# Reciprocals and layer-norm powers moved from VectorE and GpSimd to logarithm, exponential and correction steps on ScalarE and GpSimd, with new program orders

## The chip, the core and the metric

The kernel runs on one core of a Trainium2 chip. A core has five engines that run side by side, each with its own instruction queue taken in order: TensorE (PE in the profile; PEld are its weight loads), VectorE (DVE), ScalarE (ACT), GpSimd (POOL) and SyncE (SP), which here only starts DMA transfers. Engines wait for each other through semaphores. The metric is the device time of one execution in microseconds (us); lower is better.

## What is computed

The input is 32 images of 56 x 56 positions with 32 channels. A binarized 3x3 convolution is added to the image, then a linear-attention block and a mixture of experts, each behind a layer norm over the 32 channels:

```
x = x + conv(sign(batchnorm(groupnorm(x))), sign(W) * scale)
t = x as tokens                       # 3136 tokens per image
z = layernorm(t)                      # (t - mean) / sqrt(var + 1e-5)
q, k = elu(z Wq + bq) + 1, elu(z Wk + bk) + 1;  v = z Wv + bv      # 16 heads of 32
kv = sum over tokens of k*cos (x) v and of k*sin (x) v
denom = 1 / (q*cos . sum(k*cos) + q*sin . sum(k*sin) + 1e-5)       # per token and head
t = t + (q*cos . kv_cos + q*sin . kv_sin) * denom  @ dense_w + dense_b
z = layernorm(t)
t = t + sum over the 2 best of 8 experts of gate * (z We + be)
```

Two things in it matter here: `1 / sqrt(var + eps)` of both layer norms, 112 x 28 values per image each, and the reciprocal of the attention's denominator, two pieces of 128 x 224 values per image.

## The kernel before, in words

Each image is cut into seven tiles of four token groups (28 slots of 112 tokens). All work on an image is split into steps with short names, and a table `ORDER` gives each engine a list of times for each kind of step. A period is 14 units; times outside 0 to 14 mean that the step belongs to an earlier or later image than the one at hand. `iteration` sorts the table into one list per engine, so in the steady state every engine repeats a fixed list in which the steps of up to six images are interleaved. Nothing is decided at run time: an engine does its steps in that order and waits where a semaphore isn't there yet. The table also fixes which step uses which of three PSUM ring slots (`ring`) and the one shared bank (`misc`).

The steps that the change touches:

- `XC` centers the first layer norm's input on PE and ACT; `SM1` on DVE sums the squares (L993) and makes the variance `varr` (L996). `S2` and `SM2` do the same for the second layer norm, with the same line L996 for `varr`.
- `PN1` and `PN2` on POOL raise `varr` to the power -0.5 into `rstd` (L819), and multiply it into `xn` (L825). After that PE transposes `xn` (`ZT`, `ZU`, L572), ACT and DVE split it into two half-precision parts `zhl` (L717, L1007), and SP sends it through DRAM into `z`.
- `DN` and `SU` on PE make the attention's denominator, in two pieces per image; ACT adds a constant and stores it as `den` (L745).
- `RC` on DVE takes the reciprocal of `den` in place (L1032); `RC` on ACT rounds it to half precision, `r_high` (L749); `RL` on POOL stores the difference of the two (L850) into `rs`, and `RH` on ACT copies the rounded part beside it (L753).
- `R` and `RP` on PE spread `rs` over heads (L636); DVE (`R`, L1035) and, from a copy `spread_r` by ACT (L759), POOL (`RP`, L838) multiply it into `qbuf`.
- `K` and `Q` on PE (L582, L610) make keys and queries; ACT takes the exponential (L722, L727) and DVE finishes elu + 1 (L1012, L1018). `F` are the experts' products: PE (L670), gating on DVE (L1097), three pairwise sums on POOL (L877, L880, L883).

POOL's two uses of the power, and DVE's reciprocal, read before:

```
nc.gpsimd.tensor_tensor(rstd[ln][:, :], varr[ln][:, :], power[0:PT, 0:SLOTS], ALU.pow)
v.reciprocal(den[:, 0:HALFW], den[:, 0:HALFW])
act.activation(r_high[:, :], den[:, 0:HALFW], ACT.Copy)
```

## Time and profile before

| | |
|---|---|
| median of three runs | 2406.02 us (2404.33 to 2406.26) |
| the profiled execution's own time | 2404.97 us |
| its span, from first to last instruction | 2403.2 us |
| PE busy | 2183.1 us (91%) |
| DVE busy | 2062.3 us (86%) |
| POOL busy | 1839.2 us (77%) |
| ACT busy | 1516.3 us (63%) |

Busy time is the union of an engine's instructions, so overlapping ones count once. The span has three parts: a prologue and fill in which the first images enter, a steady state that repeats image by image, and a drain. The shares of the whole span mix these, so what one step is worth is read from the steady part. The TensorE clock is granted at full speed (1.00, 2.4 GHz) all through the steady part.

### The profile page before, as it was taken

How to read it: one execution, taken by the hardware profiler on the slowest of the kernel's cores; microseconds unless marked ns; L12 is line 12 of the kernel's file. 1: busy time of each engine (PE TensorE's matmuls, PEld its weight loads, DVE VectorE, ACT ScalarE, POOL GpSimd, SP SyncE). 2: the span in 40 equal slices, each digit the busy share in tenths (PEclk: the TensorE clock that was granted, in tenths of full speed). 3: DMA queues.
4: the chain of work that ended last, by engine and by line, in shares of the span. 5: the costliest groups of instructions: out<-in, count | busy, mean ns of one | idle time of the engine just before them, and what ended most of it. 6: DMA issues, size and time to landing. Idle time of an engine off the chain costs nothing.

```text
span 2403.2 us, 44296 instructions
## 1 busy us (share of the span) xinstructions
PE 2183.1 (91%) x15620; PEld 1098.5 (46%) x15620; DVE 2062.3 (86%) x2694; ACT 1516.3 (63%) x2757; POOL 1839.2 (77%) x1553
## 2 busy tenths in 40 slices
PE   5379999999999999999999999999999999999972
PEld 5224444444444444444444444444444444444441
DVE  5257899999999999999999999999999999999853
ACT  0157767667666666666667666676676766766630
POOL 0314688888888888888888888888888888888786
PEclk8589999999999999999999999999999999999985
DMA  9442323323343243344432343344322333332111
GB/s 235 121 55 39 62 50 59 68 55 65 72 71 65 55 55 68 57 60 72 72 68 59 51 65 65 52 72 72 72 61 52 58 68 54 66 65 61 28 28 34
DMA packets 485705, 156.59 MB, mean 65 GB/s; under 512 B 438688, under 2 KB 472336, under 8 KB 485360
## 3 DMA queue, kind: packets, MB, share of 16 engines
q1 hardware_dynamic: 485488, 153.75, 35.1%
q8 instruction: 129, 2.11, 0.4%
q14 instruction: 88, 0.72, 0.1%
HBM read 95.41 MB, written 51.38 MB: 61 GB/s over the span
## 4 chain that ended last, share of the span: by engine, by line
POOL 35%; PE 25%; DVE 17%; ACT 10%; issue 10%; DMA 3%; SPq 0%; POOLq 0%; ACTq 0%; DVEq 0%
POOL rstd L819 11%; POOL qbuf L838 7%; DVE qbuf L1018 6%; POOL prod L877 5%; ACT ebuf L727 4%; PE ps L619 4%; POOL xn L825 4%; PE ps L645 3%; POOL prod L880 3%; PE ps L593 3%; PE ps L610 3%; PE ps L636 2%; ACT ebuf L722 2%; POOL xcs L833 2%; PE ps L658 2%
## 5 line engine op out<-in xcount | busy, mean ns | idle before, releaser
L727 ACT ACTIVATE ebuf<-ps,small 128x896 f32<-128x896 f32 x448 | 450.3, 1005 | 163.7 <-PE ps L610 150.0
L838 POOL TENSOR_TENSOR qbuf<-spread_r,qbuf 128x896 f32<-128x896 f32 x224 | 469.4, 2096 | 94.4 <-ACT spread_r L759 94.4
L1018 DVE SCALAR_TENSOR_TENSOR qbuf<-ps,ebuf 128x896 f32<-128x896 f32 x448 | 484.9, 1082 | 58.9 <-ACT ebuf L727 58.3
L1012 DVE SCALAR_TENSOR_TENSOR kbuf<-ps,ebuf 128x1024 f32<-128x1024 f32 (+1 forms) x416 | 487.6, 1172 | 48.2 <-ACT ebuf L722 44.7
L722 ACT ACTIVATE ebuf<-ps,small 128x1024 f32<-128x1024 f32 (+1 forms) x416 | 448.0, 1077 | 116.0 <-DVE kbuf L1012 68.2
L593 PE MATMUL ps<-kbuf,xcs 128*64 128x512 f32 (+1 forms) x1600 | 440.4, 611 | 7.7 <-DVE kbuf L1012 4.0
L819 POOL TENSOR_TENSOR rstd<-varr,power 112x28 f32<-112x28 f32 x64 | 307.2, 4800 | 164.9 <-DVE varr L996 164.8
L645 PE MATMUL ps<-qbuf,gmat 128*64 128x224 f32 x3584 | 386.2, 357 | 1.6 <-DVE pbuf L1041 1.0
L645 PEld LDWEIGHTS ps<-qbuf,gmat 128*64 128x64 f32 x3584 | 248.5, 136 | 154.6 <-issue 51.3
L1097 DVE TENSOR_TENSOR prod<-ps,gate 112x1024 f32<-112x1024 f32 x224 | 273.0, 1220 | 52.2 <-PE ps L670 37.1
L877 POOL TENSOR_TENSOR prod<-prod 112x512 f32<-112x512 f32 x224 | 285.6, 1275 | 20.9 <-DVE prod L1097 20.3
L582 PE MATMUL ps<-wk,z 128*128 128x512 f16 (+1 forms) x800 | 244.2, 384 | 23.4 <-issue 14.0
L1035 DVE TENSOR_TENSOR qbuf<-ps,qbuf 128x896 f32<-128x896 f32 x224 | 243.4, 1087 | 23.3 <-PE ps L636 20.0
L636 PE MATMUL ps<-rs,sel 128*128 128x448 f16 x896 | 241.6, 358 | 20.1 <-DVE qbuf L1018 8.5
L610 PE MATMUL ps<-z,wq 128*128 128x448 f16 x896 | 246.1, 356 | 8.1 <-DVE qbuf L1018 6.9
L759 ACT ACTIVATE spread_r<-ps 128x896 f32<-128x896 f32 x224 | 205.3, 916 | 72.1 <-PE ps L636 43.7
L619 PE MATMUL ps<-qbuf,dmat 128*32 128x448 f32 x1792 | 234.8, 555 | 2.2 <-DVE qbuf L1018 1.9
L880 POOL TENSOR_TENSOR prod<-prod 112x256 f32<-112x256 f32 x224 | 163.2, 729 | 17.6
L593 PEld LDWEIGHTS ps<-kbuf,xcs 128*64 128x64 f32 (+1 forms) x1600 | 101.2, 136 | 120.6 <-issue 74.6
L670 PE MATMUL ps<-we,z 128*112 128x256 f16 x896 | 145.0, 288 | 10.4 <-DVE prod L1097 10.4
L636 PEld LDWEIGHTS ps<-rs,sel 128*128 128x128 f16 x896 | 67.5, 99 | 182.3 <-issue 63.1
L717 ACT ACTIVATE zhl<-ps 128x448 f16<-128x448 f32 (+1 forms) x128 | 63.5, 497 | 134.5 <-PE ps L572 134.5
(132 smaller groups left out, 3129.0 us busy)
## 6 DMA issues: line engine op xcount, KB each, us to landing
z<-zd SPq DMA_DIRECT2D x256, 196.0 KB, 3.8
zd<-zhl SPq DMA_DIRECT2D x64, 392.0 KB, 2.4
qbuf<-in_x SPq DMA_DIRECT2D x16, 784.0 KB, 9.5
xt<-in_x SPq DMA_DIRECT2D x256, 49.0 KB
xd<-xn SPq DMA_DIRECT2D x128, 98.0 KB, 2.9
out<-ffn SPq DMA_DIRECT2D x256, 49.0 KB
xkt<-xd SPq DMA_DIRECT2D x32, 384.0 KB, 6.6
shifted<-nat SPq DMA_DIRECT2D x128, 52.6 KB, 5.3
```

The lines of the kernel that those rows point to most:

```text
L593: mm = pe.matmul(kt_bank[64 * k:64 * k + 64, :], xcs[0:w, i, :, :].rearrange("p a c -> p (a c)"), kbuf[0:w, m.at(KS, n) % 2, DH * k:DH * k ...
L610: mm = pe.matmul(o[:, k, 0:G * PT].rearrange("p (g t) -> p g t", g=G), wq16[:, 128 * (k0 + k):128 * (k0 + k) + 128], z1[:, m.par, :, j, :] ...
L619: mm = pe.matmul(o[32 * j:32 * j + 32, 0:HW4], dmat[:, m.par, c, :, :].rearrange("p a h -> p (a h)"), qbuf[:, c, 4 * h + j, :], start=(c = ...
L636: mm = pe.matmul(o[:, k, 0:HW4], sel16[:, 128 * a:128 * a + 128], rs[:, j // 4, :], start=True, stop=True)
L645: mm = pe.matmul(o[64 * v:64 * v + 64, 0:2 * PT].rearrange("p (a t) -> p a t", a=2), gmat[:, m.par, c, :, :].rearrange("p a o -> p (a o)") ...
L722: act.activation(ebuf[0:w, 0, 0:DH * c].rearrange("p (a b) -> p a b", a=c), o[0:w, 0:c, :], ACT.Exp, bias=minus_one[0:w, :]).then_inc(kexp ...
L727: act.activation(ebuf[:, 1, 0:2 * G * PT].rearrange("p (a b) -> p a b", a=2), o[:, :, 0:G * PT], ACT.Exp, bias=minus_one).then_inc(qexp_ma ...
L819: nc.gpsimd.tensor_tensor(rstd[ln][:, :], varr[ln][:, :], power[0:PT, 0:SLOTS], ALU.pow)\
L838: nc.gpsimd.tensor_tensor(qbuf[:, 2:4, n, :], spread_r[:, :, :], qbuf[:, 2:4, n, :], ALU.mult)\
L877: nc.gpsimd.tensor_tensor(p[:, :, 0:4 * C], p[:, :, 0:4 * C], p[:, :, 4 * C:], ALU.add)\
L1012: v.scalar_tensor_tensor(kbuf[0:w, m.at(KS, n) % 2, 0:DH * c].rearrange("p (a b) -> p a b", a=c), o[0:w, 0:c, :], 1.0, ebuf[0:w, 0, 0:DH * ...
L1018: v.scalar_tensor_tensor(qbuf[:, k0:k0 + 2, j, :], o[:, :, 0:G * PT], 1.0, ebuf[:, 1, 0:2 * G * PT].rearrange("p (a b) -> p a b", a=2), AL ...
```

## The change

It replaces the reciprocal on DVE. ACT now takes the logarithm of `den` (into its unused half, named `resid`) and the exponential of its negative, which gives `r_high` directly. A new POOL step `RE` multiplies `den` by `r_high`; a new ACT step `SQ` takes the square of (1.5 minus that); `RL` on POOL subtracts 0.25 and multiplies by `r_high`. It replaces the power on POOL as well: new ACT steps `LV1` and `LV2` take logarithm, exponential and square of `varr`-sized tiles, and POOL corrects the seed with three small instructions. The program loads ACT's function table once, at the start, under a name that holds both functions. And the whole table `ORDER` is a new one, for all five engines.

```
+            nc.scalar.preload_act_table_set("natural_log_exp_and_others")
...
                     act.activation(den[:, 0:HALFW], o[:, 0:HALFW], ACT.Identity, bias=den_eps).then_inc(den_made, 1)
-                elif kind == "RC":
-                    act.wait_ge(recip_made, m.at(2, n + 1))
+                    act.wait_ge(den_made, m.at(2, n + 1))
+                    act.activation(resid, den_in, ACT.Ln).then_inc(log_made, 1)
+                    act.wait_ge(log_made, m.at(2, n + 1))
                     wait(act, qr_made, m.at(7, -3 if n == 0 else 0))
-                    act.activation(r_high[:, :], den[:, 0:HALFW], ACT.Copy).then_inc(rhigh_made, 1)
+                    act.activation(r_high[:, :], resid, ACT.Exp, scale=-1.0).then_inc(rhigh_made, 1)
+                elif kind == "SQ":
+                    act.wait_ge(resid_made, m.at(2, n + 1))
+                    act.activation(resid, resid, ACT.Square, bias=three_half, scale=-1.0).then_inc(resid_squared, 1)
+                elif kind in ("LV1", "LV2"):
+                    ln = kind == "LV2"
+                    act.wait_ge(var_made[ln], m.at(1, 1))
+                    act.activation(lnv[ln][:, :], varr[ln][:, :], ACT.Ln, scale=SEED * SEED).then_inc(seed_step[ln], 1)
+                    act.wait_ge(seed_step[ln], m.at(2, 1))
+                    act.activation(seed[ln][:, :], lnv[ln][:, :], ACT.Exp, scale=-0.5).then_inc(seed_step[ln], 1)
+                    act.wait_ge(seed_step[ln], m.at(2, 2))
+                    act.activation(newton[ln][:, :], seed[ln][:, :], ACT.Square, scale=SEED).then_inc(seed_made[ln], 1)
...
-                    pool.wait_ge(var_made[ln], m.at(1, 1))
-                    nc.gpsimd.tensor_tensor(rstd[ln][:, :], varr[ln][:, :], power[0:PT, 0:SLOTS], ALU.pow)\
+                    pool.wait_ge(seed_made[ln], m.at(1, 1))
+                    nc.gpsimd.tensor_tensor(newton[ln][:, :], newton[ln][:, :], varr[ln][:, :], ALU.mult)\
+                        .then_inc(newton_step[ln], 1)
+                    pool.wait_ge(newton_step[ln], m.at(2, 1))
+                    nc.gpsimd.tensor_scalar(newton[ln][:, :], newton[ln][:, :], -0.5 * SEED, 1.5 * SEED, ALU.mult, ALU.add)\
+                        .then_inc(newton_step[ln], 1)
+                    pool.wait_ge(newton_step[ln], m.at(2, 2))
+                    nc.gpsimd.tensor_tensor(rstd[ln][:, :], seed[ln][:, :], newton[ln][:, :], ALU.mult)\
                         .then_inc(rstd_made[ln], 1)
...
+                elif kind == "RE":
+                    pool.wait_ge(rhigh_made, m.at(2, n + 1))
+                    nc.gpsimd.tensor_tensor(resid, den_in, r_high[:, :], ALU.mult).then_inc(resid_made, 1)
                 elif kind == "RL":
-                    pool.wait_ge(rhigh_made, m.at(2, n + 1))
+                    pool.wait_ge(resid_squared, m.at(2, n + 1))
+                    nc.gpsimd.tensor_scalar(resid, resid, -0.25, None, ALU.add).then_inc(resid_series, 1)
+                    pool.wait_ge(resid_series, m.at(2, n + 1))
...
-                elif kind == "RC":
-                    dve.wait_ge(den_made, m.at(2, n + 1))
-                    v.reciprocal(den[:, 0:HALFW], den[:, 0:HALFW]).then_inc(recip_made, 1)
```

Of the table, one line each of before and of the change:

```
-        "RC": [10.80, 17.78],
+        "SQ": [8.169, 15.462],
```

Three places of the new order, in the middle of the program.

On GpSimd, from the second layer norm's power to the second piece of the attention's reciprocal; before it reads (L819 are the powers, L825 `xn`, L833 `xcs`, L838 `RP`, L877 to L883 the sums of `F`, L850 `RL`):

```order
L819 TENSOR_TENSOR rstd<-varr,power 112x28 [waits var_made2]
L825 TENSOR_TENSOR xn<-xc,rstd 112x28x31 [waits high_made2,rstd_made2]
L833 TENSOR_TENSOR xcs<-xkt,tabk 128x13x32 [waits ktx_done,xkt_in]
L833 TENSOR_TENSOR xcs<-xkt,tabk 128x13x32
L838 TENSOR_TENSOR qbuf<-spread_r,qbuf 128x2x448 [waits r_copied]
L819 TENSOR_TENSOR rstd<-varr,power 112x28 [waits var_made1]
L825 TENSOR_TENSOR xn<-xc,rstd 112x28x31 [waits xkt_out,high_made1,rstd_made1]
L877 TENSOR_TENSOR prod<-prod 112x4x128 [waits prod_made]
L880 TENSOR_TENSOR prod<-prod 112x4x64 [waits pool_add]
L883 TENSOR_TENSOR ffn<-prod 112x128 [waits pool_add]
```

and of the change the piece from the first layer norm's correction (L846, L849, L852) to `RL` (L885, L888), where L882 is `RE` and L915 to L921 are the sums of `F`:

```order
L846 TENSOR_TENSOR newton<-newton,varr 112x28 [waits seed_made1]
L849 TENSOR_SCALAR newton<-newton 112x28 [waits newton_step1]
L852 TENSOR_TENSOR rstd<-seed,newton 112x28 [waits newton_step1]
L858 TENSOR_TENSOR xn<-xc,rstd 112x28x31 [waits xkt_out,high_made1,rstd_made1]
L882 TENSOR_TENSOR den<-den,r_high 128x224 [waits rhigh_made]
L915 TENSOR_TENSOR prod<-prod 112x4x128 [waits prod_made]
L918 TENSOR_TENSOR prod<-prod 112x4x64 [waits pool_add]
L921 TENSOR_TENSOR ffn<-prod 112x128 [waits pool_add]
L885 TENSOR_SCALAR den<-den 128x224 [waits resid_squared]
L888 TENSOR_TENSOR rs<-den,r_high 128x448 [waits resid_series]
```

The power has become three instructions behind a wait for ACT's seed, and a multiply for `RE` and a small add stand where there was only the subtraction.

On ScalarE, around the first piece of the reciprocal; before (L745 stores `den`, L749 rounds it, L727 and L722 are the exponentials of `Q` and `K`, L777 is `S2`, L753 is `RH`):

```order
L745 ACTIVATE den<-ps,small 128x224 [waits r_made,misc_full]
L727 ACTIVATE ebuf<-ps,small 128x896 [waits q_made,ring_full]
L722 ACTIVATE ebuf<-ps,small 128x1024 [waits k_made,ring_full]
L749 ACTIVATE r_high<-den 128x224 [waits qr_made,recip_made]
L777 ACTIVATE sq<-xc 112x256 [waits piece_summed,centered]
L727 ACTIVATE ebuf<-ps,small 128x896 [waits q_made,ring_full]
L753 ACTIVATE rs<-r_high 64x224 [waits r_made]
```

and of the change (L760 stores `den`, L762 is the logarithm, L765 the exponential, L768 `SQ`, L804 `S2`, L742 and L737 the exponentials of `Q` and `K`, L796 and L798 `T2`, L780 `RH`):

```order
L760 ACTIVATE den<-ps,small 128x224 [waits r_made,misc_full]
L762 ACTIVATE den<-den 128x224 [waits den_made]
L765 ACTIVATE r_high<-den 128x224 [waits qr_made,log_made]
L804 ACTIVATE sq<-xc 112x256 [waits piece_summed,centered]
L742 ACTIVATE ebuf<-ps,small 128x896 [waits q_made,ring_full]
L768 ACTIVATE den<-den,small 128x224 [waits resid_made]
L737 ACTIVATE ebuf<-ps,small 128x1024 [waits k_made,ring_full]
L796 ACTIVATE t<-ps 112x256 [waits misc_full]
L798 ACTIVATE mean<-ps 112x8
L780 ACTIVATE rs<-r_high 64x224 [waits r_made]
```

ACT now does three instructions in a row for each piece, and stops once more, at L768, for GpSimd.

On VectorE, where the two variances are made in the changed order (L1035; L1032 is the first layer norm's sum, L1016 binarizes, L1051 and L1057 finish `K` and `Q`, L1071 is `R`):

```order
L1051 SCALAR_TENSOR_TENSOR kbuf<-ps,ebuf 128x1024 [waits ktx_done,kexp_made]
L1071 TENSOR_TENSOR qbuf<-ps,qbuf 128x2x448 [waits ring_full]
L1016 TENSOR_SCALAR nat<-ps,bin_a,bin_thr 128x16x28 [waits shift_in,misc_full]
L1032 TENSOR_REDUCE ssum<-sq 112x28 [waits xc_made1]
L1035 TENSOR_SCALAR varr<-ssum 112x28 [waits rstd_made1,ssum_made1]
L1051 SCALAR_TENSOR_TENSOR kbuf<-ps,ebuf 128x1024 [waits ktx_done,kexp_made]
L1035 TENSOR_SCALAR varr<-ssum 112x28 [waits rstd_made2,piece_summed]
```

The two `varr` steps, which stood apart before, are now neighbours with one step of `K` between them, and no reciprocal of `den` is in the list any more.

## Rows read from the trace of the kernel before

**Rows 1.** Windows: us, each engine's busy time (instructions), PE clock, DMA share, GB/s.

```profile
322.01:2165.80 1843.79, 1778.56 (x12962) 883.84 (x12961) 1697.82 (x2161) 1274.53 (x2322) 1538.07 (x1297) 1.00 0.36 63
```

**Rows 2.** The chain that ended last, share of the span by engine.

```profile
POOL 35%; PE 25%; DVE 17%; ACT 10%; issue 10%; DMA 3%; SPq 0%; POOLq 0%; ACTq 0%; DVEq 0%
```

**Rows 3.** Timeline of POOL: start us, us, instruction, [idle before and its end].

```profile
99.73 4.81 POOL L819 TENSOR_TENSOR rstd<-varr,power 112x28 f32<-112x28 f32 x1 [14.19 <-DVE varr L996]
...
1017.92 4.80 POOL L819 TENSOR_TENSOR rstd<-varr,power 112x28 f32<-112x28 f32 x1 [2.79 <-DVE varr L996]
...
1029.57 1.04 POOL L850 TENSOR_TENSOR rs<-den,r_high 128x448 f16<-128x448 f32 x1
...
2347.65 4.80 POOL L819 TENSOR_TENSOR rstd<-varr,power 112x28 f32<-112x28 f32 x1
```

**Rows 4.** Groups of POOL in 322.01 to 2165.80: count, busy us, mean ns, idle before.

```profile
L819 POOL TENSOR_TENSOR rstd<-varr,power 112x28 f32<-112x28 f32 x55 | 264.0, 4800 | 114.4 <-DVE varr L996 114.4
...
L880 POOL TENSOR_TENSOR prod<-prod 112x256 f32<-112x256 f32 x189 | 137.8, 729 | 14.8
...
L883 POOL TENSOR_TENSOR ffn<-prod 112x128 f32<-112x128 f32 x189 | 86.1, 455 | 14.8
...
L856 POOL TENSOR_TENSOR route<-route,first 112x224 f32<-112x224 f32 x54 | 35.8, 662 | 24.3 <-DVE route L1079 24.3
```

**Rows 5.** Groups of DVE in 322.01 to 2165.80, same columns.

```profile
L1032 DVE RECIPROCAL den<-den 128x224 f32<-128x224 f32 x54 | 83.5, 1546 | 3.5
...
L996 DVE TENSOR_SCALAR varr<-ssum 112x28 f32<-112x28 f32 x54 | 9.4, 175 | 0.9
```

**Rows 6.** Groups of the whole run, ACT and POOL, same columns.

```profile
L727 ACT ACTIVATE ebuf<-ps,small 128x896 f32<-128x896 f32 x448 | 450.3, 1005 | 163.7 <-PE ps L610 150.0 <-DVE qbuf L1018 4.2
...
L777 ACT ACTIVATE sq<-xc 112x256 f32<-112x256 f32 (+1 forms) x128 | 49.3, 385 | 3.3 <-POOL xc L843 3.3
...
L745 ACT ACTIVATE den<-ps,small 128x224 f32<-128x224 f32 x64 | 28.6, 447 | 97.3 <-PE ps L627 97.3
L749 ACT ACTIVATE r_high<-den 128x224 f16<-128x224 f32 x64 | 24.8, 387 | 2.3 <-DVE den L1032 2.3
...
L786 ACT ACTIVATE rmax<-rmax 112x28 f32<-112x28 f32 x32 | 7.2, 226 | 5.3 <-DVE rmax L1083 4.2
...
L691 ACT ACT_TABLE_LOAD x1 | 1.3, 1283 | 77.1 <-DVE nat L977 77.1
...
L807 POOL CAST wk<-qbuf 128x512 f16<-128x512 f32 x1 | 0.6, 610 | 0.1
...
L807 POOL CAST we<-qbuf 128x264 f16<-128x264 f32 x1 | 0.4, 402 | 0.1
```

**Rows 7.** Timelines of POOL and DVE: two small DVE instructions beside POOL's multiply.

```profile
1043.56 2.10 POOL L838 TENSOR_TENSOR qbuf<-spread_r,qbuf 128x896 f32<-128x896 f32 x1 [0.87 <-ACT spread_r L759]
...
1044.40 1.29 DVE L1086 TENSOR_SCALAR rmax<-rmax 112x28 f32<-112x28 f32 x1
...
2294.06 2.08 POOL L838 TENSOR_TENSOR qbuf<-spread_r,qbuf 128x896 f32<-128x896 f32 x1
...
2294.97 1.19 DVE L996 TENSOR_SCALAR varr<-ssum 112x28 f32<-112x28 f32 x1
```

**Rows 8.** Timeline of PE: a pair of half-precision matmuls and the next pair.

```profile
1004.65 0.54 PE L610 MATMUL ps<-z,wq 128*128 128x448 f16 x2
1005.03 0.59 PE L582 MATMUL ps<-wk,z 128*128 128x512 f16 x2
```

**Rows 9.** Timeline of ACT: the rounding of the reciprocal's second piece.

```profile
1022.91 0.38 ACT L749 ACTIVATE r_high<-den 128x224 f16<-128x224 f32 x1
```

**Rows 10.** Waits of DVE in 322.01 to 2165.80: us in total, times, longest.

```profile
DVE zhl L1007 <- ACT zhl L717: 30.7, 54, 0.7
```

**Rows 11.** DMA issues of the page: count, KB each, median us to landing.

```profile
z<-zd SPq DMA_DIRECT2D x256, 196.0 KB, 3.8
zd<-zhl SPq DMA_DIRECT2D x64, 392.0 KB, 2.4
```

More of the change, by code:

```diff
@@ L40 @@
 SHIFT = 2.0 ** -22
+SEED = 2.0 ** -20
 def consts():
@@ new lines @@
+        "RP": [9.550, 10.526, 13.954, 14.741, 16.566, 17.757, 19.751],
+        "SU": [7.278, 14.793],
+        "ZU": [28.800, 28.971],
+        "SQ": [8.169, 15.462],
+        "RH": [9.135, 16.038],
+        "ZT": [-11.937, -11.750],
+        "LG": [32.207],
+        "T2": [18.507, 20.524, 23.091, 23.582],
+        "KT": [5.422],
+        "G": [6.129, 6.445],
+        "S2": [20.640, 21.282, 23.931, 25.622],
+        "RT": [34.768],
+        "TB": [10.153],
+        "XC": [-15.331],
+        "LV1": [-14.661],
@@ L177 @@
+        "LV2": [27.739],
     },
     "gpsimd": {
[L179 to L188 removed]
+        "T2": [26.594, 28.821, 31.310, 31.424],
+        "CS": [1.025, 5.702],
+        "F": [43.115, 44.033, 46.026, 47.335, 48.673, 49.626, 51.552],
@@ L189 @@
+        "RE": [15.148, 21.260],
+        "RL": [15.567, 22.015],
+        "RP": [17.835, 19.338, 20.399, 23.348, 23.795, 24.239, 26.040],
+        "PN2": [33.892],
+        "PN1": [-7.102],
+        "OUT": [51.840],
+        "RF": [38.053, 39.705],
+        "GT": [41.548],
     },
     "sync": {
-        "CS": [-17.68, -12.90],
-        "CV": [-23.27],
-        "XT": [-36.85],
-        "ZU": [19.44],
-        "OUT": [39.11],
-        "ZT": [-14.92],
+        "ZU": [30.164],
+        "ZT": [-11.720],
@@ L197 @@
+        "CS": [-19.462, -11.347],
+        "OUT": [46.666],
+        "CV": [-19.963],
+        "XT": [-33.745],
     },
@@ L278, in build @@
         bn_gain = small[:, 11:12]
+        three_half = small[:, 13:14]
         bin_a = sb("bin_a", [128, B])
@@ L295, in build @@
         varr = [sb(f"varr{k}", [PT, SLOTS]) for k in (1, 2)]
+        lnv = [sb(f"lnv{k}", [PT, SLOTS]) for k in (1, 2)]
+        seed = [sb(f"seed{k}", [PT, SLOTS]) for k in (1, 2)]
+        newton = [sb(f"newton{k}", [PT, SLOTS]) for k in (1, 2)]
         rstd = [sb(f"rstd{k}", [PT, SLOTS]) for k in (1, 2)]
@@ L308, in build @@
         den = sb("den", [128, HW4])
+        den_in, resid = den[:, 0:HALFW], den[:, HALFW:HW4]
         r_high = sb("r_high", [128, HALFW], F16)
@@ L396, in build @@
         den_made = sem("den_made")
-        recip_made = sem("recip_made")
+        log_made = sem("log_made")
+        resid_made = sem("resid_made")
+        resid_squared = sem("resid_squared")
+        resid_series = sem("resid_series")
+        seed_step = [sem(f"seed_step{k}") for k in (1, 2)]
+        seed_made = [sem(f"seed_made{k}") for k in (1, 2)]
+        newton_step = [sem(f"newton_step{k}") for k in (1, 2)]
         rhigh_made = sem("rhigh_made")
@@ L846, in step @@
                         .then_inc(centered, 1)
+                elif kind == "RE":
+                    pool.wait_ge(rhigh_made, m.at(2, n + 1))
+                    nc.gpsimd.tensor_tensor(resid, den_in, r_high[:, :], ALU.mult).then_inc(resid_made, 1)
                 elif kind == "RL":
-                    pool.wait_ge(rhigh_made, m.at(2, n + 1))
+                    pool.wait_ge(resid_squared, m.at(2, n + 1))
+                    nc.gpsimd.tensor_scalar(resid, resid, -0.25, None, ALU.add).then_inc(resid_series, 1)
+                    pool.wait_ge(resid_series, m.at(2, n + 1))
                     both = [128, 2, HALFW]
                     nc.gpsimd.tensor_tensor(rs[:, n, :].rearrange("p (c t) -> p c t", c=2),
-                                            den[:, 0:HALFW].unsqueeze(1).to_broadcast(both),
-                                            r_high[:, :].unsqueeze(1).to_broadcast(both), ALU.subtract).then_inc(r_made, 1)
+                                            resid.unsqueeze(1).to_broadcast(both),
+                                            r_high[:, :].unsqueeze(1).to_broadcast(both), ALU.mult).then_inc(r_made, 1)
                 elif kind == "RF":
```

31 lines of the change are left out of this document (4 added, 27 removed), and 64 rows, old and new, of the table ORDER.

## The prediction

> **What bounds the kernel now.** I read the windows first. The span is a fill of 322 us, a steady state from 322.01 to 2165.80 [rows 1], and a drain of 237 us. The steady window runs from the start of one power L819 to that of another and holds 55, first and last included [rows 4]; with two to an image that is 27 images in 1843.79 us, 68.29 us each. This is where nearly all of the time is.
>
> Per image (busy time of the window over 27) PE is busy 65.87 us, DVE 62.88, POOL 56.97, ACT 47.20 [rows 1]. PE looks full, but a burst counts as busy until its last result: two matmuls of `Q` last 0.54 us, and the next burst starts 0.38 us after the first did [rows 8]. So up to 0.16 us behind each short burst is no work, and PE's share doesn't prove PE to be the bound. DVE has 5.41 us without work per image.
>
> Then the chain: POOL holds 35% of it, more than PE or DVE [rows 2], with less busy time than either. The timeline says why. POOL stands still until DVE's `varr` is there, 2.79 us before one of the powers, then spends 4.80 us in it [rows 3]; over the steady part that wait is 114.4 us, 4.2 us per image [rows 4]. Behind the second power the attention's reciprocal queues: ACT rounds it at 1022.91 for 0.38 us [rows 9], but `RL` L850 starts at 1029.57 [rows 3], 6.3 us later, because the rest of the power, `xn` and two sums of `F` stand in front. DVE, PE and POOL bound the period together, and POOL's lateness is handed on: DVE waits 30.7 us, 1.14 per image, for `zhl`, the first thing made from `xn` [rows 10].
>
> **The change, part by part, per image.**
>
> *DVE.* Two reciprocals of 1.546 us go [rows 5]: 62.88 - 3.09 = 59.79 us. Nothing is added, but a new wait is likely. In the steady part `varr` takes 0.175 us [rows 5], always with POOL standing still for it. Where POOL was in the middle of L838, the same small instruction took 1.19 us and ended 0.02 us after POOL's did; L1086, of the same kind, takes 1.29 us beside L838 and ends 0.03 us after it [rows 7]. In the changed program POOL no longer stands still there, since three ACT steps lie between `varr` and the correction. So each of the two `varr` costs between 0 and a whole L838 (2.10 us) more; the rows give 1.0 where the two meet. I take half, as POOL has idle time and short instructions too: +1.0, DVE 60.8, with 59.8 and 64.0 as ends. The Trainium skill says the same in its GPSIMD Engine Reference, Specifications: GpSimd's SBUF interface is shared with VectorE, and the two contend for some of VectorE's instructions. The trace agrees with the 1.29 us of L1086.
>
> *POOL.* Two powers go, 9.60 us. Added per layer norm: two products and one scale-and-add of 112 x 28. No row has them. POOL's sums take 455 ns for 128 columns and 729 for 256 [rows 4], 2.14 ns per column, so 28 columns extrapolate to 0.24 us; the casts, with one input, take 402 ns for 264 columns and 610 for 512 [rows 6], so 28 columns give 0.20. Together 0.69, and about 0.85 with two waits on its own results. Bounds: 0 and three times 0.455. Added per piece of the reciprocal: `RE`, 0.66 by L856 of 112 x 224 [rows 4], and the add of 0.25, 0.37 by the casts. `RL`'s product has the shape of the subtraction it replaces. Sum: 56.97 - 9.60 + 1.37 + 2.06 = 50.8 us, and the 4.2 us of waiting become usable.
>
> *ACT.* The exponential replaces the rounding one for one. Added per piece: a logarithm, 0.387 us as L749, and a square with a bias, 0.447 as L745; per layer norm three of 112 x 28 at 0.226, as L786 [rows 6]. Sum: 47.20 + 1.67 + 1.36 = 50.2 us, still the least loaded engine; it lies in ACT's 21 us of idle time. The exception is `SQ`: ACT stops there for `RE` on POOL, and the exponentials of `K` and `Q`, for which DVE waits, queue behind it. For the first piece the order puts one `S2` and one `Q` between, 0.385 + 1.005 = 1.4 us of cover [rows 6]; `RE` with its hand-off takes 0.75, so it may start 0.6 us late for nothing. One round of `F` stands before it on POOL (0.73 + 0.46 and a sum of twice the columns, some 1.3, by [rows 4]). I charge 0.5 us per image.
>
> The reciprocal's own path doesn't get shorter: `den`, logarithm, exponential, `RE`, square, add, product against `den`, reciprocal, rounding, subtraction. The gain is that no 4.80 us instruction stands in the queue any more. A layer norm gets 4.80 - 0.68 (ACT) - 0.85 (POOL) - some 0.1 = 3.2 us shorter.
>
> *A function table.* One load took 1.28 us, once [rows 6]; the change's order lists one as well. The Trainium skill, ScalarE: Activation LUTs, Table sets, speaks against mixing functions (about 2.7 us for each switch of sets) but names one set that holds both exp and ln. By that the price is nothing, which is what I sum.
>
> *The new order.* It moves everything, and I take no gain for it. On SP the transfers are the same. One place changes what waits: `ZU`'s write and read now stand right behind `CS`, which waits for `xn` of the first layer norm, so the experts' `z` lands some 2.4 + 3.8 = 6.2 us [rows 11] and the issue of `CS` after that `xn`. What needs it is `LG` on PE, which the table puts nine steps behind `ZT`, itself made from that `xn`; `xn` comes early on POOL, with `ZT` thirteen steps of PE behind `SU`. I charge nothing; without that cover it would be a stop of up to 6 us per image, more than the whole gain.
>
> **The sum.** Of DVE's 5.41 us without work I take away the 1.14 behind `xn` and keep 4.27: 60.8 + 4.3 + 0.5 = 65.6 us per image, 2.7 less than 68.29. Over 27 images that is 73 us. In the fill POOL idled 14 us for the first image's `varr` [rows 3] and the power was on the path; for the first two images 3.2 us each, 6. In the drain the last power (2347.65, [rows 3]) and the one before it are on the path, 6, and one more full period gives 3. In all 73 + 6 + 9 = 88 us off the profiled execution's 2404.97: 2317. The median of the runs is 1 us above that execution, so I say 2318 us, 3.7% faster.
>
> **Rivals.**
>
> *Deeper gain (0.19).* With POOL and DVE both lighter, DVE's waits shrink too, until PE is the bound. At 59.8 + 3.0 = 62.8 us the saving is 5.5 x 27 + 15 = 163 us: 2242; at 64.1 (no port wait, no stop at `SQ`) 113 + 15: 2277. For it: most of PE's bursts hide some waiting. Against: PE would have to run closer to its matmuls than it ever does.
>
> *POOL's collisions eat it (0.17).* Both `varr` meet an L838 and pay 2.1 us each; DVE is at 64.0, and with 4.3 us of waits the period is 68.3: only fill and drain gain, 2390. At half of that it is 2350. This is the page's rule at full price; the two rows at 1.2 and 1.3 us speak for it, POOL's 15 us of idle time per image (65.6 - 50.8) and its many short sums against.
>
> *Slower: ACT is held at `SQ` (0.11).* The second piece's `RE` stands behind both layer norms' corrections and a round of `F`. If ACT waits there, `K`'s exponentials are late, DVE starves, and PE fills its three ring slots and stops. It decides from 3.3 us of stop per image (88 / 27) beyond what is charged; two stops of 2.5 us give 65.6 + 5.0 = 70.6, 2404.97 + 62 - 15 = 2452. For it: two new hand-offs from ACT to POOL and back in a queue that had one. Against: for the second piece four steps of other work stand between, twice as many as for the first.
>
> *The tables are switched after all (0.02).* Four pairs per image with two loads each, 8 x 1.28 = 10.3 us on ACT: about 2450 or more. The order's single load speaks against it.
>
> **How the numbers follow.** The forecast (64.4 to 66.8 us per image, 2285 to 2352) has 0.51. It and the deeper gain are faster: 0.70. Of the collisions' 0.17 I give 0.13 to faster and 0.04 to within 0.2% (about 5 us, which is what a measurement of this kernel can tell); 0.01 more for an exact draw. Slower holds 0.11 + 0.02 less that 0.01: 0.12. The range runs from inside the deeper case to the end of the collisions, 2255 to 2396, and leaves out about 2 in 10.
>
> **What would show it.** Right: no RECIPROCAL of `den` on DVE, POOL near 51 us and ACT near 50 per image, small POOL products at 0.2 to 0.3 us, one table load, a period of 64.4 to 66.8, and POOL's share of the chain well below 35%. `varr` near 0.7 us on average shows the collisions; 1.2 or more, at their full price. ACT idle before the square with bias, for POOL, shows the slower case. Wrong: POOL's small instructions cost far more than extrapolated, or a period above 68.

## The result, and the profile after

The changed kernel takes 2370.51 us (median of 4 runs, 2363.26 to 2374.62), against 2406.14 us of the kernel before beside it (2404.33 to 2407.95): a ratio of 0.9849, 95% interval 0.9823 to 0.9874. It is faster by 1.5%, where 3.7% was forecast. The profiled execution took 2370.66 us with a span of 2368.9.

First the page of the changed kernel: busy time by engine, and the chain that ended last, to be read against [rows 2].

```profile
PE 2199.1 (93%) x15620; PEld 1101.4 (46%) x15620; DVE 1943.0 (82%) x2631; ACT 1612.5 (68%) x3077; POOL 1654.6 (70%) x1809
...
PE 61%; POOL 16%; DVE 6%; DMA 5%; ACT 5%; issue 4%; SPq 2%; POOLq 0%; ACTq 0%; DVEq 0%
```

POOL's share has fallen from 35% to 16% and PE's has risen from 25% to 61%. A kernel whose lateness ran through POOL has become one that waits for TensorE's own work, and for transfers, which hold 5% and SP's queue 2% more.

The windows of the changed kernel: fill, the same 27 images, drain (columns as in [rows 1]).

```profile
0.00:321.62 321.62, 244.83 (x1509) 126.36 (x1510) 204.79 (x330) 159.18 (x289) 103.41 (x109) 0.84 0.48 97
321.62:2147.12 1825.50, 1794.51 (x12958) 886.71 (x12957) 1596.27 (x2106) 1356.32 (x2592) 1381.79 (x1512) 0.99 0.35 64
2147.12:2368.90 221.78, 159.71 (x1155) 88.28 (x1155) 141.89 (x197) 96.98 (x197) 169.42 (x188) 0.84 0.18 41
```

Against [rows 1] the fill is 0.4 us shorter (322.01), the steady part 18.3 (1843.79) and the drain 15.6 (237.39): 34.3 in all. Per image the period went from 68.29 to 67.61 us. DVE's busy time is 59.12, ACT's 50.23 and POOL's 51.18 us, near the 59.8 (60.8 with the collisions that were charged), 50.2 and 50.8 forecast. So the work shrank as it was worked out, and three quarters of the steady gain are missing nevertheless.

The new instructions, groups of the whole run on POOL, DVE and ACT:

```profile
L888 POOL TENSOR_TENSOR rs<-den,r_high 128x448 f16<-128x448 f32 x64 | 66.4, 1038 | 5.3
L885 POOL TENSOR_SCALAR den<-den 128x224 f32<-128x224 f32 x64 | 49.2, 768 | 27.5 <-ACT den L768 27.5
L882 POOL TENSOR_TENSOR den<-den,r_high 128x224 f32<-128x224 f32 x64 | 39.1, 612 | 14.1 <-ACT r_high L765 14.1
L846 POOL TENSOR_TENSOR newton<-newton,varr 112x28 f32<-112x28 f32 x64 | 15.6, 244 | 211.9 <-ACT newton L776 211.9
...
L1035 DVE TENSOR_SCALAR varr<-ssum 112x28 f32<-112x28 f32 x64 | 11.6, 181 | 1.1
...
L772 ACT ACTIVATE lnv<-varr 112x28 f32<-112x28 f32 x64 | 13.7, 213 | 5.5 <-DVE varr L1035 5.5
...
L694 ACT ACT_TABLE_LOAD x1 | 1.3, 1283 | 0.7 <-PEq L1180 0.7
```

The tables are loaded once. `varr` stays at 0.18 us on average (0.175 in [rows 5]); the longest of the 64 takes 0.55, beside POOL's multiply L871. POOL runs nothing during 62 of them, as in the kernel before: it still stands still ahead of the first correction L846, now for ACT's seed, 163.9 us in the steady part or 6.1 per image. POOL has 16 us to spare per image, but `xn` comes behind this wait; no run here shows what the wait costs.

The period is not one number any more. Before, it was 68.28 to 68.30 us in nearly every image; after, it runs from 66.60 to 69.10 (66.47 for the last). Below are windows of one of the long periods (1339.48 to 1405.55 us, without its first 2.6) and of one of the short ones, then the chain through the start of the long one.

```profile
1339.48:1405.55 66.07, 65.00 (x464) 31.71 (x462) 56.47 (x76) 49.22 (x95) 48.85 (x52) 0.97 0.37 65
657.03:723.64 66.61, 65.86 (x481) 32.70 (x481) 59.14 (x79) 50.25 (x96) 51.16 (x56) 1.00 0.37 65
```

```profile
1345.03 1.66 POOL xn L858
1347.07 0.54 SPq L510
1347.65 0.57 SPq L510
1348.27 1.97 SPq L510
1350.33 3.12 DMA zd<-zhl
1354.77 4.67 DMA z<-zd
1359.58 1.58 PE ps L678 x28
...
1362.98 0.75 PE ps L650 x2
1363.72 0.75 PE ps L624 x2
1364.47 0.75 PE ps L650 x2
1365.22 1.42 PE ps L607 x2
```

The short period has PE busy for 65.86 of 66.61 us. The chain of the long one starts with what the new order on SP did: `xn` of the first layer norm, then the issue of `CS` (L510), and only then the write and read of the experts' `z`, for which `LG` (L678) waits on TensorE. The wait itself is short, 0.31 us here; in the whole steady part it is this (us in total, times, longest):

```profile
PE ps L678 <- DMA z<-zd: 3.0, 8, 0.7
```

Behind `LG`'s narrow matmuls the same pairs of matmuls that hold 0.38 to 0.54 us of the chain elsewhere hold 0.75. The granted clock of that stretch:

```profile
1359.58:1361.90 2.32, 2.32 (x34) 2.08 (x34) 1.11 (x3) 1.29 (x2) 2.09 (x2) 1.00 0.22 51
1361.90:1365.30 3.40, 3.40 (x17) 1.76 (x17) 2.18 (x4) 1.79 (x5) 2.69 (x2) 0.61 1.12 225
1365.30:1368.70 3.40, 3.40 (x21) 1.42 (x22) 2.13 (x5) 1.62 (x3) 0.00 (x0) 0.89 1.32 139
```

It falls from 1.00 to 0.61, that is to 1.2 GHz for most of the second window. The steady part before had a mean of 1.00 [rows 1]; the one after has 0.99. Windows of all 27 periods show where that comes from: the eight longest, 68.66 to 69.10 us, have a mean clock of 0.98 (0.97 in the window above, which is shorter), the nineteen others, up to 68.20, have 1.00. Seven of the eight falls come soon behind an `LG` that waited for z; the eighth comes behind one with only 0.10 us of idle time before it, and the shortest of the eight waits, 0.18 us, is not followed by one. The eight long periods lie 17.8 us above eight of 66.62, and the waits are no more than 3.0 of that.

### The profile page after: what moved, and what is told of

Same layout as the page of the kernel before. It is cut to its first block, busy times and chain, and to the rows that moved or that the text cites. A ratio compares the mean times of both kernels' runs of the same rounds, so it can differ in the third digit from the quotient of the medians.

```text
span 2368.9 us, 44809 instructions
## 1 busy us (share of the span) xinstructions
PE 2199.1 (93%) x15620; PEld 1101.4 (46%) x15620; DVE 1943.0 (82%) x2631; ACT 1612.5 (68%) x3077; POOL 1654.6 (70%) x1809
## 4 chain that ended last, share of the span: by engine, by line
PE 61%; POOL 16%; DVE 6%; DMA 5%; ACT 5%; issue 4%; SPq 2%; POOLq 0%; ACTq 0%; DVEq 0%
PE ps L607 14%; PE ps L659 9%; PE ps L650 7%; PE ps L596 6%; PE ps L624 4%; PE ps L633 4%; POOL prod L915 3%; ACT ebuf L737 2%; PE ps L672 2%; DVE kbuf L1051 2%; PE ps L579 2%; PE ps L670 2%; PE ps L684 2%; PE ps L574 2%; PE ps L678 2%
## 5 line engine op out<-in xcount | busy, mean ns | idle before, releaser
L742 ACT ACTIVATE ebuf<-ps,small 128x896 f32<-128x896 f32 x448 | 450.6, 1006 | 251.7 <-PE ps L624 223.8
L1057 DVE SCALAR_TENSOR_TENSOR qbuf<-ps,ebuf 128x896 f32<-128x896 f32 x448 | 487.0, 1087 | 100.8 <-ACT ebuf L742 98.0
L1051 DVE SCALAR_TENSOR_TENSOR kbuf<-ps,ebuf 128x1024 f32<-128x1024 f32 (+1 forms) x416 | 490.4, 1179 | 93.6 <-ACT ebuf L737 75.8
L871 POOL TENSOR_TENSOR qbuf<-spread_r,qbuf 128x896 f32<-128x896 f32 x224 | 469.2, 2095 | 65.6 <-ACT spread_r L786 63.2
L737 ACT ACTIVATE ebuf<-ps,small 128x1024 f32<-128x1024 f32 (+1 forms) x416 | 449.4, 1080 | 86.8 <-PE ps L596 68.5
L659 PEld LDWEIGHTS ps<-qbuf,gmat 128*64 128x64 f32 x3584 | 238.3, 137 | 158.5 <-issue 74.5
L915 POOL TENSOR_TENSOR prod<-prod 112x512 f32<-112x512 f32 x224 | 285.2, 1273 | 3.4 <-DVE prod L1133 3.4
L1071 DVE TENSOR_TENSOR qbuf<-ps,qbuf 128x896 f32<-128x896 f32 x224 | 243.3, 1086 | 35.9 <-PE ps L650 32.6
L650 PE MATMUL ps<-rs,sel 128*128 128x448 f16 x896 | 235.2, 363 | 26.3 <-ACT rs L780 25.9
L786 ACT ACTIVATE spread_r<-ps 128x896 f32<-128x896 f32 x224 | 204.8, 914 | 71.3 <-POOL qbuf L871 36.9
L633 PE MATMUL ps<-qbuf,dmat 128*32 128x448 f32 x1792 | 213.6, 547 | 3.0 <-DVE pbuf L1077 3.0
L607 PEld LDWEIGHTS ps<-kbuf,xcs 128*64 128x64 f32 (+1 forms) x1600 | 88.8, 136 | 161.2 <-issue 129.7
L846 POOL TENSOR_TENSOR newton<-newton,varr 112x28 f32<-112x28 f32 x64 | 15.6, 244 | 211.9 <-ACT newton L776 211.9
L650 PEld LDWEIGHTS ps<-rs,sel 128*128 128x128 f16 x896 | 75.6, 104 | 175.1 <-issue 142.3
L624 PEld LDWEIGHTS ps<-z,wq 128*128 128x128 f16 x896 | 72.5, 99 | 175.7 <-issue 92.5
```

Of the source, the lines that this page charges most:

```text
L607: mm = pe.matmul(kt_bank[64 * k:64 * k + 64, :], xcs[0:w, i, :, :].rearrange("p a c -> p (a c)"), kbuf[0:w, m.at(KS, n) % 2, DH * k:DH * k ...
L624: mm = pe.matmul(o[:, k, 0:G * PT].rearrange("p (g t) -> p g t", g=G), wq16[:, 128 * (k0 + k):128 * (k0 + k) + 128], z1[:, m.par, :, j, :] ...
L633: mm = pe.matmul(o[32 * j:32 * j + 32, 0:HW4], dmat[:, m.par, c, :, :].rearrange("p a h -> p (a h)"), qbuf[:, c, 4 * h + j, :], start=(c = ...
L650: mm = pe.matmul(o[:, k, 0:HW4], sel16[:, 128 * a:128 * a + 128], rs[:, j // 4, :], start=True, stop=True)
L659: mm = pe.matmul(o[64 * v:64 * v + 64, 0:2 * PT].rearrange("p (a t) -> p a t", a=2), gmat[:, m.par, c, :, :].rearrange("p a o -> p (a o)") ...
L737: act.activation(ebuf[0:w, 0, 0:DH * c].rearrange("p (a b) -> p a b", a=c), o[0:w, 0:c, :], ACT.Exp, bias=minus_one[0:w, :]).then_inc(kexp ...
```

## The experiments

All ratios are against runs of the kernel before on the same chip. "Per image" is the mean of 24 steady images of the profiled run (from one `PN2` on POOL to the same one 24 images later): 68.29 us before, 67.72 after.

### What made the period long after: z's place

**z first.** In SP's table:

```
-        "ZU": [30.164],
+        "ZU": [22.400],
```

> The changed kernel with one number moved: on SyncE's queue the write and read of the second layer norm's z stand ahead of the write of the x slices again (ZU at 22.400 instead of 30.164). Theory A (TensorE's own work sets the period, about 66.6 us per image as in the shortest periods after, and the late z adds about 1.0 us per image on average to 67.6): every steady period near 66.6, 27 x 1.0 = 27 us less, about 2343 us (2335 to 2352), no 1.2 GHz stretch in the steady part, and hardly a wait of L678 for z's transfer. Theory B (VectorE's load and its small waits set the period, as forecast): z's place is hidden, no change, 2365 to 2376. Theory C (transfers vary by themselves, wherever they stand in the queue): the long periods stay, 2360 to 2376.

Measured: 2351.15 us (2345.11 to 2358.81), ratio 0.9777 (0.9754 to 0.9799), 19.4 us below the changed kernel. Of 27 periods sixteen are within 0.03 us of 66.62, and the others reach 68.1. TensorE waits for z no more, though `LG` stands at the same place of its list, and the clock is 1.00 in the steady part:

```profile
322.00:2147.00 1825.00, 1800.18 (x13094) 891.80 (x13089) 1616.02 (x2129) 1371.95 (x2619) 1400.14 (x1533) 1.00 0.35 64
```

PE is busy 98.6% of it. Theory A's range holds, 8 us above its number because some long periods stay (66.84 per image on average, not 66.62); their clock is 1.00, and their cause stays open. So z's place cost 0.8 us per image on average (1825.50 us for the 27 images after, 1803.94 here), less by TensorE's waits, which are at most 3.0 us in all, than by the eight periods with a fall of the clock, which are gone with them.

**A quarter of TensorE's numerator left out** (on top of z first):

```
-                    for c in range(CH):
+                    for c in range(3):
```

> As the run with z first, and TensorE's numerator products (L659) run over three of the four column groups: a quarter of the numerator is left out, 32 matmuls per image and some 2.9 us of TensorE's time per image (389.5 us / 32 / 4 = 3.0); no other engine's instructions change. Theory A (TensorE sets the period): the period falls by most of it, until VectorE or the chain through it binds: 64 to 65 us, 2275 to 2310 us. Theory B (VectorE with its waits sets it): less than 0.5 us per image below the run with z first, so above 2328.

Measured: 2321.0 us (2314.72 to 2326.4), ratio 0.9649 (0.963 to 0.9668); 66.10 per image, shortest 65.10. The gain over z first is 30 us, in the steady part 0.74 us per image of the 3.0 taken away (two periods of 71.4 and 69.8, with a mean clock under 1.00, are in the mean). Both theories miss: it is more than B allows and less than A wanted, 2310 at most. TensorE's work does set the period with z first, but what binds next stands only some 1.5 us behind it (66.60 against 65.10).

**A wait taken out of TensorE.** With z first, one wait of TensorE is left in every image. Waits of PE in that kernel from 322 to 2147 us (us in total, times, longest), then POOL's timeline of the chain that makes the rows it waits for:

```profile
PE ps L650 <- ACT rs L780: 18.1, 27, 0.7
```

```profile
1637.53 0.61 POOL L882 TENSOR_TENSOR den<-den,r_high 128x224 f32<-128x224 f32 x1
1638.74 0.77 POOL L885 TENSOR_SCALAR den<-den 128x224 f32<-128x224 f32 x1 [0.60 <-ACT den L768]
1639.59 1.04 POOL L888 TENSOR_TENSOR rs<-den,r_high 128x448 f16<-128x448 f32 x1
```

The edit lets TensorE do a T2 step meanwhile:

```
-        "RP": [10.037, 10.696, 14.397, ...
+        "RP": [10.045, 10.696, 14.397, ...
```

> The run with z first, and on TensorE the first spread product of the next reciprocals (L650, which waits 0.7 us in every image for the rows that ScalarE copies after the new reciprocal's chain) put behind the T2 step that stood right after it (0.9 us of other matmuls). Theory A (TensorE sets the period of 66.62 and this wait is its last large one): 0.6 to 0.7 us less per image, 66.0, about 2333 us (2325 to 2342). Rival (another chain stands right behind it, as the 65.3 us with a quarter of the numerator gone suggests, or what waits for the spread loses as much): within 0.2 us per image of the run with z first, 2345 to 2353.

Measured: 2338.64 us (2335.36 to 2341.77), ratio 0.972 (0.9706 to 0.9733), 12.5 us below z first; 66.46 per image, shortest 66.24 but for the last. The time lies in theory A's range, but only 0.38 of the 0.6 to 0.7 us per image came back. The wait is gone (in the same stretch the list of PE's waits now holds only 3.8 us of issue). This is the fastest version of this study that computes everything: 67.7 us below the kernel before.

**The same quarter left out of the kernel before.** The edit is the same, in L642 and L647 there.

> The kernel before with TensorE's numerator products over three of the four column groups: a quarter of the numerator is left out, 32 matmuls and some 2.9 us of TensorE's time per image. Theory A (before, the chain through GpSimd's powers and VectorE set the period, TensorE only as far as it is met on the way): the period falls by less than 1 us, 2375 to 2400 us. Rival (TensorE already set it before): by 2 us and more per image, under 2350.

Measured: 2425.78 us (2422.07 to 2438.51), ratio 1.0086 (1.0058 to 1.0114). With less work the kernel is slower, which neither side had. The shortest period is 67.33, 0.95 below the 68.28 of before, as theory A said; but others are 69.6 to 71.3. Timeline of PE in one of these, and windows with the granted clock:

```profile
700.20 1.36 PE L645 MATMUL ps<-qbuf,gmat 128*64 128x224 f32 x12
703.73 0.84 PE L603 MATMUL ps<-p,ktsb 128*32 128x66 f32 x32 [2.17 <-DVE qbuf L1035]
704.70 0.78 PE L656 MATMUL ps<-eye_mean,t1b 128*112 128x132 f32 x2
```

```profile
700.00:703.40 3.40, 1.56 (x14) 0.77 (x12) 3.37 (x4) 1.17 (x3) 2.08 (x1) 1.00 0.62 148
703.40:706.80 3.40, 2.94 (x43) 2.69 (x43) 2.50 (x7) 2.81 (x20) 1.76 (x3) 0.60 1.32 177
706.80:710.20 3.40, 3.40 (x17) 2.96 (x16) 1.40 (x2) 1.46 (x3) 1.28 (x2) 0.50 0.73 65
```

TensorE, relieved, stands still for 2.17 us, narrow matmuls follow, and the clock falls to 0.60 and 0.50, which is 1.2 GHz for most of these two windows. Windows of all 27 periods show the same: the twelve of 69.55 us and more have a mean clock of 0.95 or 0.98, the fifteen others, 67.33 to 68.36, have 1.00. So before, TensorE was not the bound, and relieving it cost more in clock than it gave.

### What each part of the change is worth

The two new parts and the new orders were tried apart. The old parts use the old instructions at the old places of the table or, in the new orders, at the places of the new steps that they replace.

**Both new parts, old orders.** The tables of before, with these new lines for ACT and POOL:

```
+        "SQ": [9.06, 17.30],
+        "LV1": [-12.935],
+        "LV2": [27.01],
...
+        "RE": [17.50, 21.00],
```

> The new reciprocals and powers in the orders of the kernel before (the new steps put at their places in those orders). Theory A (the steady gain is the removed waits of VectorE and GpSimd, bounded by TensorE): 2355 to 2385. Rival (the gain is that of the new orders): 2396 or more, as before.

Measured: 2504.86 us, ratio 1.0415 (1.0399 to 1.043). Neither: the new arithmetic in the old orders loses 99 us.

**Both old parts, new orders.** POOL's `pow` and VectorE's `RC`, tables of after without `LV1`, `LV2` and `RE`.

> The reciprocals and powers of the kernel before (VectorE's reciprocal, GpSimd's power) in the new orders. Theory A (two separate contributions): about 2385, between 2370 and 2400. Rival (the orders were only good with the new arithmetic, which moved GpSimd's blocks): 2400 or more, with z's place costing nothing any longer.

Measured: 2607.18 us, ratio 1.085 (1.0831 to 1.0869); 75.08 per image. The rival's side, and far beyond it; and z's place costs more there, not nothing. Waits of DVE and PE in this kernel:

```profile
DVE rmax L1062 <- PE ps L664: 124.0, 32, 10.8
...
PE ps L664 <- DMA z<-zd: 77.1, 31, 11.2
```

TensorE (L664 is `LG` here) waits for z in 31 of 32 images, and VectorE's routing waits for the logits. The chain is `pow`, `xn`, `CS` on SP, z, `LG`, with 4.80 us of power at its head. In 26 of the 27 periods the mean clock is below 1.00 (0.93 to 0.98).

**The same with z first.**

> The old reciprocals and powers in the new orders (2607 us as run before), with the second layer norm's z ahead of the x slices on SyncE's queue. Theory A (what makes the old arithmetic so slow in the new orders is z's place behind slices that wait for two powers): most of the 201 us above the kernel before goes, 2390 to 2450. Rival (the other orders, made for short steps, hold it too): above 2520.

Measured: 2461.32 us, ratio 1.0226 (1.0209 to 1.0243). 146 of the 201 us are z's place; the other 55 stay, so A names the larger part and its number is missed by 11. The clock is 1.00 in every period now, so in these 146 us, too, a part is the clock's.

**Only the power back, new orders.**

```
-                    nc.gpsimd.tensor_tensor(newton[ln][:, :], newton[ln][:, :], varr[ln][:, :], ALU.mult)\
...
+                    nc.gpsimd.tensor_tensor(rstd[ln][:, :], varr[ln][:, :], power[0:PT, 0:SLOTS], ALU.pow)\
```

> The changed kernel with GpSimd's power back for the two layer norms (the logarithm-exponential seed and its three corrections left away), the new reciprocals and the new orders kept, z still behind the x slices on SyncE's queue. Theory A (the new orders and the late z hang on the short layer-norm step: with 4.80 us of power twice per image, x's slices are made later, z waits behind them on the queue, and L678 on TensorE waits for z; so nearly all of the 236 us that both old parts cost in the new orders comes back with the power): 2540 to 2610 us. Rival (the two old parts cost about alike there): 2470 to 2510. Rival (TensorE sets the period and covers it): 2375 to 2400.

Measured: 2537.51 us, ratio 1.0543 (1.0525 to 1.0562). 167 us come back with the power, just under A's lower end.

**Only the reciprocal back, new orders**, and **the same with z first**:

```
+                    v.reciprocal(den[:, 0:HALFW], den[:, 0:HALFW]).then_inc(log_made, 1)
```

> The changed kernel with VectorE's two RECIPROCALs per image back and the short high-part copy and subtraction (the steps by logarithm, exponential and square left away), layer norms and orders as after. Theory A (TensorE sets the period; 3.1 us more of VectorE are covered but for a part of a wait each): 2365 to 2400 us. Theory B (VectorE sets the period, as forecast): 27 x 3.1 = 84 us more, about 2455. Rival (the two old parts cost about alike in the new orders): 2470 to 2510.

> The run with z first, and VectorE's reciprocals back. Theory A (TensorE sets the period there and the reciprocal's 3.1 us on VectorE cost only what its wait adds, as 67.51 against 66.62 us in the shortest periods shows): 0.9 us per image above the run with z first, 2370 to 2380, so no more than 6 us below the run with the reciprocal back and z late. Theory B (VectorE sets it): 3 us per image above, 2430 or more.

Measured: 2376.51 us, ratio 0.9877 (0.9861 to 0.9892), an interval that overlaps the changed kernel's; and 2386.64 us, ratio 0.9913 (0.9899 to 0.9928). With z late, the new reciprocals are worth 6 us, no more than can be measured. With z first they are worth 35. Theory A's range holds with z late and is missed by 7 us with z first. Waits of PE in the kernel of the first of these runs:

```profile
PE ps L596 <- DVE prod L1127: 28.5, 29, 1.0
```

The old reciprocal costs TensorE about 1 us per image through what queues behind it on VectorE; the shortest periods are 67.5. Theory B, by which all of the 3.1 us come back, fails. What also fails is that z first could only help: here it is 10 us slower, with a series of periods of 68 to 69 us in the second half. The clock is 1.00 in these, and their cause stays open.

**Only the power new, old orders; only the reciprocal new, old orders.** The code of the two runs above, the tables of before with the lines of the part that is new.

> The kernel before with the layer-norm powers alone replaced by the seeds on ScalarE and the corrections on GpSimd; VectorE's reciprocal and the old orders stay. Theory A (the power's 4.80 us on GpSimd stood on the path that set the period, and the loss of 99 us with both new parts in the old orders comes from the longer reciprocal chain): 2330 to 2395 us. Rival (the seeds are late in ScalarE's old order, so that GpSimd waits longer than the power took): 2440 or more.

> The kernel before with the reciprocals alone replaced (logarithm, exponential and square on ScalarE, product, addition and product on GpSimd); GpSimd's power and the old orders stay. Theory A (its chain crosses between ScalarE and GpSimd twice more, and in the old orders each side waits for the other with other work queued behind): slower than before, 2440 to 2520 us. Rival (VectorE's 3.1 us set the period, so they come back as gain): under 2390.

Measured: 2387.46 us, ratio 0.9919 (0.9905 to 0.9932), for the power; 2510.23 us, ratio 1.0429 (1.0414 to 1.0443), for the reciprocal. Both as theory A said. The power's gain is 19 us, but only 0.41 per image in the steady part (67.88), where POOL had 8 us less to do. Below is ACT's and POOL's timeline of the second piece of the reciprocal in the slower kernel, from the store of `den` (L758) to the copies of its rows (L778):

```profile
1204.84 0.45 ACT L758 ACTIVATE den<-ps,small 128x224 f32<-128x224 f32 x1 [0.35 <-PE ps L639]
...
1215.41 0.47 ACT L766 ACTIVATE den<-den,small 128x224 f32<-128x224 f32 x1
...
1217.90 0.79 ACT L778 ACTIVATE rs<-r_high 64x224 f16<-64x224 f16 x2 [2.02 <-POOL rs L880]
```

```profile
1212.70 0.61 POOL L874 TENSOR_TENSOR den<-den,r_high 128x224 f32<-128x224 f32 x1
...
1216.83 1.04 POOL L880 TENSOR_TENSOR rs<-den,r_high 128x448 f16<-128x448 f32 x1
```

13.1 us lie between the starts of the store and of the copies. In ACT's timeline of the kernel before the same two starts are 11.5 us apart for the second piece and 4.1 for the first:

```profile
1224.07 0.45 ACT L745 ACTIVATE den<-ps,small 128x224 f32<-128x224 f32 x1 [0.35 <-PE ps L627]
...
1235.57 0.79 ACT L753 ACTIVATE rs<-r_high 64x224 f16<-64x224 f16 x2 [0.82 <-POOL rs L850]
...
1262.81 0.45 ACT L745 ACTIVATE den<-ps,small 128x224 f32<-128x224 f32 x1 [2.62 <-PE ps L627]
...
1266.91 0.79 ACT L753 ACTIVATE rs<-r_high 64x224 f16<-64x224 f16 x2
```

So the new chain is 1.6 us longer for the second piece. For the first, which takes 5.3 us as in the timeline further below, it is 1.2 longer. A part of the loss is the clock: eleven of the 27 periods, 72.67 to 73.04 us, have a mean clock of 0.98, the sixteen others take 71.0 us at 1.00.

**Other places in the old orders**, for the reciprocal alone and for both parts:

```
-        "SQ": [9.06, 17.30],
+        "SQ": [9.06, 16.90],
...
-        "RE": [17.50, 21.00],
-        "RL": [17.51, 21.54],
+        "RE": [17.50, 20.80],
+        "RL": [17.51, 21.20],
```

> The run with the new reciprocals alone in the old orders (2510 us), with the second half's steps at other places: the residual product on GpSimd ahead of the feed-forward sum that stood before it, the last two steps ahead of the next such sum, and ScalarE's square ahead of the copy of z that waits for TensorE. The same instructions. Theory A (the loss is queueing: the steps stand behind work that is late): rows are copied some 2.7 us earlier in every image, 27 x 2.7 = 73 us less, 2420 to 2460. Rival (the longer chain costs this wherever it stands): 2495 or more.

> Both new parts in the old orders (2505 us as run before), with the same three moves. Theory A (queueing): 2400 to 2455, as the reciprocals' run falls, with the power's 19 us on top. Rival (the longer chain itself): 2485 or more.

Measured: 2480.53 us, ratio 1.0306 (1.0289 to 1.0323), and 2465.8 us, ratio 1.0242 (1.0226 to 1.0257). Between the bounds of both theories: 30 and 39 us come back. Timeline of ACT with the moves, reciprocal alone, first and second piece:

```profile
1225.48 0.45 ACT L758 ACTIVATE den<-ps,small 128x224 f32<-128x224 f32 x1 [2.62 <-PE ps L639]
...
1230.76 0.79 ACT L778 ACTIVATE rs<-r_high 64x224 f16<-64x224 f16 x2
1256.21 0.45 ACT L758 ACTIVATE den<-ps,small 128x224 f32<-128x224 f32 x1 [0.35 <-PE ps L639]
...
1266.91 0.79 ACT L778 ACTIVATE rs<-r_high 64x224 f16<-64x224 f16 x2
```

The second piece now takes 10.7 us instead of 13.1, which is less than the 11.5 of the kernel before; the first takes 5.3, as it did without the moves. The clock is 1.00 in every period. So of the 29 us that the steady part of the reciprocal's run got back, some 19 are the eleven slow periods, and some 10 are the step from 71.02 to 70.63 us in all the others. The period is still 2.3 us above 68.29, though only the first piece's rows are later than before, by 1.2 us. TensorE's waits are 4.0 us per image, against 2.1 in the kernel before; which link makes them is not shown.

### The table of it

Medians in us; rows are the arithmetic, columns the orders.

| | old orders | new orders | new orders, z first |
|---|---|---|---|
| both old | 2406 | 2607 | 2461 |
| power new | 2387 | 2377 | 2387 |
| reciprocal new | 2510 | 2538 | not run |
| both new | 2505 (2466 with the moves) | 2371 | 2351 |

No part pays by itself as it does with the others. The new orders alone cost 201 us, the new reciprocals alone 104, and only the powers gain in every column: 19 in the old orders (5 beside new reciprocals), 231 in the new (167 beside new reciprocals), 75 with z first.

## Why the prediction was wrong

**Right: the sizes.** POOL's small products take 0.24 us (0.24 extrapolated), the scale-and-add 0.21 (0.20), `RE` 0.61 (0.66), the logarithms and squares 0.21 to 0.48. Only the add of 0.25 was mis-sized: 0.77 us instead of 0.37. The three busy times came out within 0.7 us, if the 1.0 us that was put on VectorE for collisions is left out. The stop at `SQ` was charged with 0.5 us and is 0.7 for the first piece (the 0.68 us of ACT before L768, for POOL's `RE`, in the kernel with z first); for the second there is none. There was no second table load, and next to none of the collisions with `varr` for which 1.0 us was charged: at 0.18 us the rival of the collisions is out. But the premise of that charge, that POOL no longer stands still there, was wrong: POOL runs nothing during 62 of the 64 `varr`, so the case was hardly put to the test. The Trainium skill (GPSIMD Engine Reference, Specifications) has GpSimd and VectorE contend for a shared interface, for some of VectorE's instructions; [rows 7] agree, and after the change the longest `varr`, 0.55 us, is the one beside L871.

**Wrong: the period as VectorE's load plus its waits** ("60.8 + 4.3 + 0.5 = 65.6"). It failed in three places. A reading ahead of it was wrong, too: the power of [rows 3] had ended at 1022.72, before ACT began to round at 1022.91 [rows 9], so what stood in front of `RL` was `xn` and two rounds of `F`, and no part of the power. And the 4.2 us per image that POOL waited ahead of the powers did not become usable: ahead of the corrections it waits 6.1.

1. *The new period was summed from VectorE.* The sentence that PE's share doesn't prove it to be the bound was right for the kernel before: with a quarter of the numerator gone, the period there fell by 0.95 us at best. But the sum never asked how long TensorE's own work is, once nothing else is late, and came out below the 65.87 us that PE was busy per image [rows 1]. The shortest periods after are 66.6 us with PE busy for 65.86 of them, 1 us above the forecast; z first brings most images there, and without the wait for the reciprocal's rows it is 66.2. VectorE's waits were taken to stay at 4.3 us; in fact its idle time rose to 8.5 us (67.61 - 59.12), so 3.8 us less work on it moved the period by 0.68.

2. *SP's new order was charged at nothing* ("without that cover it would be a stop of up to 6 us per image"). The place was named, and the way in which it costs was not. The nine steps of PE between `ZT` and `LG` do cover most of it: z lands 12.8 us after `xn` in the long period shown (1346.69 to 1359.44; the write and read alone were put at 6.2), and TensorE waits for it eight times in 27 images, 3.0 us in all. What was left out is the clock. Eight periods hold a stretch at 1.2 GHz, seven of them right behind such a wait, and they are 17.8 us longer than eight of 66.62. Moving z alone takes away the waits and these stretches and gives back 19.4 us of the median, 0.8 per image in the steady part. With both old parts back the cover is gone: TensorE waits for z in 31 of 32 images, 77.1 us in all.

3. *The longer chain of the reciprocal was noted and not charged* ("the reciprocal's own path doesn't get shorter"). VectorE's two instructions were counted as 3.1 us of gain, and the two extra hand-offs as 0.5 us of loss. Alone in the old orders the exchange loses 104 us; there the rows come 1.2 and 1.6 us later after `den` is stored, and eleven periods hold a fall of the clock that the moves in the old orders take away. What the remaining 2.3 us per image hang on stays open. In the new orders the exchange gains between nothing measurable and 35.

**Fill and drain.** Between the marks that the forecast used, the starts of `PN2` on POOL, the fill gained 0.4 us where 6 were forecast and the drain 15.6 where 9 were. Much of that is the mark: the next step, `PN1`, starts 13.07 us later before and 7.19 after, so by it the fill is 6.3 us shorter (335.08 against 328.81) and the drain 10.1. Together they are 16 against 15 forecast. So the missing 54 us (34.3 of 88) are all in the steady part, 18.3 of 73: 2 us per image, of which item 1 explains about 1 (66.62 against 65.6) and item 2 about 0.8. The last 0.2 is the periods that stay long with z first, and is open.

**The new orders** were "taken for no gain". They are no gain and no loss but a condition: with the old arithmetic they cost 201 us, without them the new arithmetic costs 99. The power is what they hang on (167 of the 236 us from both old to both new).

## What to carry to other kernels

When an engine off the bound is relieved, sum the period also from the next engine's own work with no wait in it, and take that as the floor: here it stood 1.7 us below the old period (68.28 against 66.60), whatever VectorE saved. A step of a queue that is put behind another which waits for late work inherits that wait; price it at its full size until the trace shows what covers it. Look at the granted clock period by period: here waits of 3.0 us in all came with eight periods that were 17.8 us longer. An order written out by hand belongs to the arithmetic that it was made for: exchange them together, and don't add up gains that were measured apart.
